# Attention projections placed by SyncE and ScalarE together, x tiles issued first, rows of minus one filled by Pool

## The chip, the core and the metric

The kernel runs on one core of a Trainium2 chip. The core has five engines that run their own instruction streams: TensorE (PE in the profile), VectorE (DVE), ScalarE (ACT), Pool (POOL) and SyncE (SP, which here only issues DMAs). A DMA that an engine issues stands in that engine's stream; the transfer itself is done by sixteen DMA engines that all issuers share. The metric is device time in microseconds of one execution, lower is better.

## What is computed

The reference chains four blocks over a hidden state of 2048 tokens by 1024 features, each with a layer norm before and behind it and a residual. The change is in the third, grouped-query causal attention over two sequences of 1024 tokens (b = 2, t = 1024). Cut to what matters:

```python
q = jnp.dot(x, Wq).reshape(b, t, H, HD).transpose(0, 2, 1, 3)
kv = jnp.dot(x, Wkv).reshape(b, t, G, 2, HD).transpose(2, 3, 0, 1, 4)
scores = jnp.einsum('bhqd,bhkd->bhqk', q, k)
scores = jnp.where(causal[None, None], -jnp.inf, scores)
weights = jax.nn.softmax(scores * (1.0 / HD ** 0.5), axis=-1)
ctx = jnp.einsum('bhqk,bhkd->bhqd', weights, v)
```

There are 32 query heads of 32 features and 8 key and value groups; the kernel works through 16 head groups of four query heads each, eight for either sequence. Everything is float32 in and out; products are made from a high and a low part of each operand, which is why each projected matrix exists as `qh` (high) and `ql` (low).

## The kernel before

The program is four stages (StageA to StageD) with a barrier of all engines between them. Each engine's stream is written out by hand, and waits are on counting semaphores (`Sig`). The third stage, StageC, is the one that the diff touches. It works like this.

**Opening.** SyncE loads sixteen x tiles (`sp_x`, L1638) into four buffers, tile u as soon as tile u-4's buffer is free. TensorE transposes each (L1762) and multiplies it for V (L1784 to L1786); ScalarE takes the high part (L1961) and copies V (L1967), VectorE makes the low part (L2119, L2122). Then come the projections, the `JOBS`: K0, K1, query groups 0, 1 and 2 ahead of the loop, the other fifteen (queries 3 to 15, K2, K3) inside it. A job has two parts of 512 columns. For a part TensorE does 24 matmuls (L1808 to L1810), ScalarE casts the high part into `c_qh` (L1974), VectorE writes the low part into `c_ql` or `c_cH` (L2131), and then the part has to be *placed*: 4 heads x 3 row blocks of 32 x 512 are copied by twelve DMAs into `c_K` (L1654) or `c_Q` (L1665), from where the heads' matmuls read them. Between jobs SyncE loads the next weights (`sp_w`, L1622), ScalarE casts them (L1943 in the opening, L1950 in quarters in the loop) and VectorE splits them (L2091, L2098).

Rows 96 of `c_K` must hold -1: VectorE writes them with two memsets (L2166, L2167) once V is complete, since the weights of V lie in the even heads of `c_K` until then; `c_K`'s row 96 times the stored row maximum in `c_Q` subtracts the maximum inside the score matmul.

**Maxima.** For each of 16 head groups o there are 48 maxima: a matmul (`pe_amax`, L1832) into one of three turning PSUM banks and a reduction on VectorE (L2142, L2146). The first 60 of them run while the last two projections of the opening do; the first waits until both parts of query group 0 and of K0 and K1 are placed.

**Loop.** 768 slots, 48 for each o. In slot S TensorE makes score S (`pe_score`, L1848) into one of three banks, maximum S+60, now and then three matmuls of a job, and a product with V (L1863); ScalarE makes the exponential (L2010) and frees the bank; Pool masks (L2225) and adds up rounds (L2240); VectorE does the maximum. A finished head is evacuated by ScalarE (L2023, L2028), and SyncE moves its sums through memory (`sp_finish`, L1682 to L1698) for a reciprocal on VectorE (L2151) and a multiplication on Pool (L2205). The table `JOBS` gives, for each job in the loop, the slots of its matmuls and the two slots from which its parts are placed; it is written by hand and the change doesn't touch it. The third stage's streams on SyncE and ScalarE are in `sp` and `act`.

An issue on SyncE or ScalarE waits for its semaphores in the stream of its engine, so what stands behind it waits too.

## Time and profile before

| | |
|---|---|
| median of 3 executions | 2426.3 us (2423.89 to 2428.33) |
| the profiled execution | 2424.34 us, span 2422.6 us |
| TensorE busy | 2162.4 us, 89% |
| VectorE busy | 1430.3 us, 59% |
| ScalarE busy | 918.8 us, 38% |
| Pool busy | 903.1 us, 37% |
| granted TensorE clock, mean | 0.947 |

Times in the rows are in us from the start of the span, durations in us or ns as marked. PE is TensorE's matmuls and PEld its weight loads, which overlap them; SPq and ACTq are DMAs issued by SyncE and ScalarE, where the duration is that of the issue and not of the transfer. The granted clock is a share of the full 2.4 GHz. A bracket behind a row is the engine's idle time before it and what ended it.

### The profile page before, as it was taken

To read this page: it belongs to the slowest core of one execution; us is meant where nothing else is said; L and a number is where in the kernel's file an instruction comes from. 1 tells how busy PE (TensorE), PEld (TensorE's weight loads), DVE (VectorE), ACT (ScalarE), POOL (GpSimd) and SP (SyncE) were. 2 spreads that over 40 slices of the span, in tenths; PEclk is the share of its full clock that TensorE was granted. 3 is DMA by queue.
4 is the path that set the end of the run, shared out by engine and by line. 5 is a ranking of instruction groups with operands and counts; after the bars stand their busy time and mean duration, and the time that the engine had idled before them with its cause. 6 is when DMAs were issued, how large, how long until landed. Compare 5 with 4: busy or idle time off the path is not lost.

```text
span 2422.6 us, 31281 instructions
## 1 busy us (share of the span) xinstructions
PE 2162.4 (89%) x11064; PEld 1530.2 (63%) x11064; DVE 1430.3 (59%) x3245; ACT 918.8 (38%) x1675; POOL 903.1 (37%) x761
## 2 busy tenths in 40 slices
PE   4899965699999978879999899999988699999998
PEld 4655534588888868755556555655543487667676
DVE  7866766577777653366766566676662156543333
ACT  4654643233332322215554455455555222221111
POOL 1344664444444420004565454556655222110000
PEclk9899987899999988979999999999987899999999
DMA  5220446112221127431223622322221544434332
GB/s 166 73 91 1 145 137 192 67 70 70 79 70 70 70 87 269 123 80 35 76 63 89 193 67 62 90 75 65 54 68 59 192 174 167 137 121 150 111 114 95
DMA packets 139570, 249.28 MB, mean 103 GB/s; under 512 B 26885, under 2 KB 69765, under 8 KB 139191
## 3 DMA queue, kind: packets, MB, share of 16 engines
q1 hardware_dynamic: 130711, 230.51, 30.1%
q10 hardware_dynamic: 8704, 16.78, 2.1%
q8 instruction: 88, 1.44, 0.3%
q14 instruction: 67, 0.55, 0.1%
HBM read 139.48 MB, written 76.02 MB: 89 GB/s over the span
## 4 chain that ended last, share of the span: by engine, by line
PE 62%; POOL 12%; DVE 10%; issue 5%; DMA 3%; ACT 3%; SPq 2%; POOLq 0%; DVEq 0%; ACTq 0%
POOL c_S L2240 10%; PE PS L2425 5%; PE PS L2382 4%; PE PS L2383 4%; PE PS L2386 4%; PE PS L1848 3%; PE PS L1069 3%; PE PS L1070 3%; PE PS L1071 3%; PE PS L1832 3%; PE PS L1863 3%; PE PS L1102 2%; PE PS L1104 2%; PE PS L1103 2%; DVE PS L2146 2%
## 5 line engine op out<-in xcount | busy, mean ns | idle before, releaser
L2010 ACT ACTIVATE c_P<-PS 128x512 f32<-128x512 f32 (+3 forms) x768 | 359.8, 495 | 366.9 <-PE PS L1848 338.0
L2240 POOL TENSOR_TENSOR c_S<-c_S,c_P 128x2048 f32<-128x2048 f32 (+6 forms) x111 | 317.0, 2864 | 73.7 <-DVE c_S L2112 66.6
L1832 PE MATMUL PS<-c_K,c_Q 96*128 96x512 f32 (+3 forms) x768 | 281.6, 377 | 45.9 <-DVE cst L2146 23.6
L1848 PE MATMUL PS<-c_Q,c_K 97*128 97x512 f32 (+3 forms) x768 | 284.5, 384 | 2.5 <-ACT c_P L2010 2.5
L1848 PEld LDWEIGHTS PS<-c_Q,c_K 97*128 97x128 f32 x768 | 149.9, 198 | 162.7 <-ACT c_P L2010 73.1
L2142 DVE TENSOR_REDUCE cst<-PS 128x1 f32<-128x512 f32 x256 | 176.1, 688 | 109.3 <-PE PS L1832 109.0
L1832 PEld LDWEIGHTS PS<-c_K,c_Q 96*128 96x128 f32 x768 | 152.1, 198 | 110.5 <-DVE cst L2146 57.6
L2225 POOL TENSOR_SCALAR_AFFINE_SELECT c_P<-c_P 128x512 f32<-128x512 f32 x128 | 81.6, 638 | 335.9 <-ACT c_P L2010 335.9
L1863 PE MATMUL PS<-c_P,c_V 128*32 128x512 f32 (+3 forms) x1536 | 172.3, 522 | 27.2 <-POOL c_P L2225 15.3
L2146 DVE CUSTOM_DVE_ANT_0 PS<-PS,maskw 128x128 f32<-128x128 f32 (+3 forms) x256 | 127.1, 505 | 85.3 <-PE PS L1832 83.9
L2382 PE MATMUL PS<-c_xth,d_xh 128*128 128x512 f32 x384 | 157.6, 410 | 19.2 <-DVE d_xl L2497 19.2
L2146 DVE CUSTOM_DVE_ANT_0 PS<-PS,maskw,cst 128x128 f32<-128x128 f32 (+3 forms) x256 | 142.9, 558 | 51.4 <-PE PS L1832 35.0
L199 POOL TENSOR_TENSOR maskw<-maskw,mhalf 128x1 f32<-128x1 f32 x64 | 36.6, 572 | 363.1 <-DVE maskw L168 363.1
L1069 PE MATMUL PS<-b_w13h,b_xsh 128*128 128x460 f32 (+1 forms) x384 | 149.0, 388 | 15.8 <-DVE b_xsl L1274 15.5
L1301 DVE SCALAR_TENSOR_TENSOR b_pr<-b_g,b_a 128x460 f32<-128x460 f32 x192 | 160.6, 872 | 1.6
L1193 ACT ACTIVATE b_g<-PS 128x460 f32<-128x460 f32 x96 | 52.9, 553 | 273.2 <-PE PS L1076 273.2
L2383 PE MATMUL PS<-c_xtl,d_xh 128*128 128x512 f32 x384 | 152.9, 398 | 0.0
L1395 POOL TENSOR_TENSOR b_gp<-b_g 128x230 f32<-128x230 f32 x96 | 84.8, 884 | 163.2 <-DVE b_g L1286 163.2
L1070 PE MATMUL PS<-b_w13l,b_xsh 128*128 128x460 f32 (+1 forms) x384 | 144.6, 376 | 0.0
L1071 PE MATMUL PS<-b_w13h,b_xsl 128*128 128x460 f32 (+1 forms) x384 | 143.7, 374 | 0.0
L1286 DVE TENSOR_TENSOR b_g<-b_g,PS 128x460 f32<-128x460 f32 x96 | 60.5, 630 | 117.2 <-ACT b_g L1193 117.2
L1808 PE MATMUL PS<-c_xth,c_wh 128*128 128x512 f32 x304 | 125.7, 414 | 4.2 <-DVE c_ql L2131 2.0
(282 smaller groups left out, 4844.1 us busy)
## 6 DMA issues: line engine op xcount, KB each, us to landing
a_xin<-in_x SPq DMA_DIRECT2D x32, 512.0 KB, 4.3
c_Q<-c_qh SPq DMA_DIRECT2D x256, 64.0 KB, 2.0
d_x<-scr SPq DMA_DIRECT2D x32, 512.0 KB, 3.9
scr<-a_xin SPq DMA_DIRECT2D x16, 512.0 KB, 5.5
scr<-a_hid SPq DMA_DIRECT2D x16, 512.0 KB, 3.0
b_xn<-scr SPq DMA_DIRECT2D x16, 512.0 KB, 5.7
b_x<-scr SPq DMA_DIRECT2D x16, 512.0 KB, 4.8
scr<-b_x SPq DMA_DIRECT2D x16, 512.0 KB, 2.6
```

Source lines behind the costliest of these rows:

```text
L1069: e.matmul(o, self.xsh[:, par, i, :], wh[:, v, i, :], start=i == 0, stop=False)
L1070: e.matmul(o, self.xsh[:, par, i, :], wl[:, v, i, :], start=False, stop=False)
L1071: e.matmul(o, self.xsl[:, par, i, :], wh[:, v, i, :], start=False, stop=False)
L1832: e.matmul(bank[:, 0:hi - lo], self.Q4[0:96, 4 * (o % 3) + g, 128 * t:128 * t + 128], self.K4[0:96, HEADS[o % 8], lo:hi], start=True, stop ...
L1848: e.matmul(self.k.bank(i % 3)[:, 0:hi - lo], self.K4[0:97, HEADS[o % 8], 128 * kt:128 * kt + 128], self.Q4[0:97, 4 * (o % 3) + g, lo:hi], ...
L1863: m = e.matmul(k.bank(5)[32 * g:32 * g + 32, lo - 512 * half:512], self.V[:, kt, o // 8, HEADS[o % 8], :], P[:, g, 0:hi - lo], start=kt == ...
L2010: e.activation(self.P[:, R % 3, g, 0:hi - lo], self.k.bank(i % 3)[:, 0:hi - lo], ACT.Exp, scale=SCALE).then_inc(self.exp_s.s, 1)
L2142: e.tensor_reduce(m, r, AX, ALU.max).then_inc(self.mx_s.s, 1)
L2146: e.tensor_tensor_reduce(out=r, in0=r, in1=self.maskw[:, 512 - n:512], scale=1.0, scalar=m if lo > 0 else -3.0e38, op0=ADD, op1=ALU.max, a ...
L2240: m = e.tensor_tensor(S[:, gs, 512 - n:512], S[:, gs, 512 - n:512], P[:, gs, 0:n], ADD)
L2382: e.matmul(o, h, wh[:, c, cols], start=c == 0, stop=False)
L2383: e.matmul(o, h, wl[:, c, cols], start=False, stop=False)
```

## The change

- SyncE issues x tile 15 and the weights for job 3 before it places any part of K0 (before, K0's first part stood between x tiles 14 and 15).
- A placement of a part is split for the jobs of the opening (n < 5) and for K2, 7, K3 and 11 in the loop: SyncE issues the six DMAs of heads 0 and 1, ScalarE the six of heads 2 and 3 (`place`, `act_place`, `shared`). The other jobs stay with SyncE. In the opening ScalarE issues the first part's six behind its cast of the second part, and the second part's six behind the next weights' cast; in the loop at the same slot as SyncE.
- The rows of minus one are written by Pool at the start of the stage (odd heads) and after V (even heads); SyncE's placement of K1 waits for V alone, and the first score waits for both memsets.

```diff
--- before.py
+++ after.py
@@ -1638,17 +1638,29 @@
         e.dma_start(self.xin[u % 4], self.xn_src[128 * t:128 * t + 128, :]).then_inc(self.k.ldx[u % 4].s, 16)
 
     def sp_place(self, e, n, part):
+        self.place(e, n, part, range(2) if self.shared(n) else range(4))
+
+    def act_place(self, e, n, part):
+        if self.shared(n):
+            self.place(e, n, part, range(2, 4))
+
+    @staticmethod
+    def shared(n):
+
+        return n < 5 or JOBS[n][0] in ("K2", 7, "K3", 11)
+
+    def place(self, e, n, part, heads):
         what = JOBS[n][0]
         c = slice(512 * part, 512 * part + 512)
         e.wait_ge(*self.qlo_s(2 * n + part + 1))
         if what in ("K0", "K1", "K2", "K3"):
             first = (1, 0, 0, 1)[int(what[1])]
             if what == "K1":
-                e.wait_ge(*self.given_s(3))
+                e.wait_ge(*self.vmm_s(16))
             elif what != "K0":
                 e.wait_ge(*self.score_s(192 if what == "K2" else 384))
                 e.wait_ge(*self.amax_s(192 if what == "K2" else 384))
-            for g in range(4):
+            for g in heads:
                 j, s = 2 * g + first, slice(32 * g, 32 * g + 32)
                 for r, q in ((0, self.qh[s, part, :]), (32, self.qh[s, part, :]), (64, self.low(n, part)[s, :])):
                     e.dma_start(self.K4[r:r + 32, j, c].bitcast(F32), q.bitcast(F32)).then_inc(self.k4[part].s, 16)
@@ -1659,7 +1671,7 @@
         if o >= 3:
             e.wait_ge(*self.score_s(48 * (o - 2)))
             e.wait_ge(*self.amax_s(48 * (o - 2)))
-        for g in range(4):
+        for g in heads:
             q, s = 4 * (o % 3) + g, slice(32 * g, 32 * g + 32)
             for r, x in ((0, self.qh[s, part, :]), (32, self.low(n, part)[s, :]), (64, self.qh[s, part, :])):
                 e.dma_start(self.Q4[r:r + 32, q, c].bitcast(F32), x.bitcast(F32)).then_inc(self.placed[part].s, 16)
@@ -1717,11 +1729,10 @@
             self.sp_x(e, u)
             if u == 11:
                 self.sp_w(e, 3)
-            if u >= 14:
-                self.sp_place(e, 0, u - 14)
         self.sp_w(e, 4)
-        for part in range(2):
-            self.sp_place(e, 1, part)
+        for n in (0, 1):
+            for part in range(2):
+                self.sp_place(e, n, part)
         self.sp_w(e, 5)
         for n in (2, 3):
             for part in range(2):
@@ -1843,6 +1854,8 @@
         i = 48 * o + 4 * r + g
         if r == 0 and g == 0:
             e.wait_ge(*self.mrow[o % 2](o // 2 + 1))
+        if i == 0:
+            e.wait_ge(*self.given_s(2))
         if i >= 3:
             e.wait_ge(*self.exp_s(i - 2))
         e.matmul(self.k.bank(i % 3)[:, 0:hi - lo], self.K4[0:97, HEADS[o % 8], 128 * kt:128 * kt + 128],
@@ -2040,16 +2053,21 @@
                 self.act_v(e, u - 3)
             if u in (12, 13):
                 self.act_job(e, 0, u - 12)
+            if u in (14, 15):
+                self.act_place(e, 0, u - 14)
             if 6 <= u < 14:
                 self.act_x1(e, 2 * u - 12)
                 self.act_x1(e, 2 * u - 11)
         for n in range(1, 5):
             for part in range(2):
                 self.act_job(e, n, part)
+                if part == 1:
+                    self.act_place(e, n, 0)
                 if n == 4 and part == 0:
                     self.act_mrow(e, 0)
             if n < 4:
                 self.act_w(e, n + 3)
+            self.act_place(e, n, 1)
         for o in range(16):
             for s, (r, g) in enumerate(SLOTS):
                 S = 48 * o + s
@@ -2064,6 +2082,8 @@
                     self.act_evac(e, 2 * o, 0)
                 if S in self.evac_at:
                     self.act_job(e, *self.evac_at[S])
+                if S in self.place_at:
+                    self.act_place(e, *self.place_at[S])
                 for n, q in self.split_at.get(S, ()):
                     self.act_w4(e, n + 1, q)
                 for q in range(4):
@@ -2157,15 +2177,11 @@
             if u == 0:
                 self.dve_w(e, 0)
                 self.dve_w(e, 1)
-                e.memset(self.maskw[:, 0:384], 0.0).then_inc(self.given_s.s, 1)
+                e.memset(self.maskw[:, 0:384], 0.0)
             if u in (6, 12):
                 self.dve_w(e, 2 if u == 6 else 3)
             if u in (12, 13):
                 self.dve_job(e, 0, u - 12)
-        e.wait_ge(*self.vmm_s(16))
-        e.memset(self.K4[96:97, 0:8:2, :].bitcast(F32), -1.0).then_inc(self.given_s.s, 1)
-        e.memset(self.K4[96:97, 1:8:2, :].bitcast(F32), -1.0).then_inc(self.given_s.s, 1)
-        e.wait_ge(*self.given_s(3))
         for n in (1, 2):
             for part in range(2):
                 self.dve_job(e, n, part)
@@ -2217,6 +2233,9 @@
     def pool(self, e):
 
         S, adds = self.S, 0
+        e.memset(self.K4[96:97, 1:8:2, :].bitcast(F32), -1.0).then_inc(self.given_s.s, 1)
+        e.wait_ge(*self.vmm_s(16))
+        e.memset(self.K4[96:97, 0:8:2, :].bitcast(F32), -1.0).then_inc(self.given_s.s, 1)
         for o in range(16):
             for r, (kt, lo, hi) in enumerate(ROUNDS):
                 P, n = self.P[:, (12 * o + r) % 3, :, :], hi - lo
```

Line numbers of the changed kernel are up to 19 higher; its placements are L1666 and L1677, its cast of `c_qh` L1987, its exponentials L2023.

SyncE's stream where the x tiles end and K0's first part is placed, before (`c_cH` and `c_cS` are two of the four x buffers here, `c_raw` the raw weights):

```order
L1638 DMA c_xin<-scr 128x1024 x2
L1638 DMA c_cH<-scr 128x1024
L1654 DMA c_K<-c_qh 32x512 x2
L1654 DMA c_K<-c_ql 32x512
L1654 DMA c_K<-c_qh 32x512 x2
L1654 DMA c_K<-c_ql 32x512
L1654 DMA c_K<-c_qh 32x512 x2
L1654 DMA c_K<-c_ql 32x512
L1654 DMA c_K<-c_qh 32x512 x2
L1654 DMA c_K<-c_ql 32x512
L1638 DMA c_cS<-scr 128x1024
```

and now:

```order
L1638 DMA c_xin<-scr 128x1024 x2
L1638 DMA c_cH<-scr 128x1024
L1638 DMA c_cS<-scr 128x1024
L1622 DMA c_raw<-in_wq 128x8x128
L1666 DMA c_K<-c_qh 32x512 x2
L1666 DMA c_K<-c_ql 32x512
L1666 DMA c_K<-c_qh 32x512 x2
L1666 DMA c_K<-c_ql 32x512
```

The last x tile and a weight load stand ahead of the placements, and a part is six issues instead of twelve.

ScalarE's stream at the end of the opening, before (`c_mT` are the transposed maxima of head group 0):

```order
L1974 CAST c_qh<-PS 128x512 x2
L1943 CAST c_wh<-c_raw 128x1024
L1974 CAST c_qh<-PS 128x512
L1980 CAST c_mT<-PS 32x128
L1974 CAST c_qh<-PS 128x512
L2010 ACT_TABLE_LOAD
L2010 ACTIVATE c_P<-PS 128x512 x4
```

and now:

```order
L1987 CAST c_qh<-PS 128x512
L1677 DMA c_Q<-c_qh 32x512
L1677 DMA c_Q<-c_ql 32x512
L1677 DMA c_Q<-c_qh 32x512 x2
L1677 DMA c_Q<-c_ql 32x512
L1677 DMA c_Q<-c_qh 32x512 x2
L1677 DMA c_Q<-c_cH 32x512
L1677 DMA c_Q<-c_qh 32x512 x2
L1677 DMA c_Q<-c_cH 32x512
L1677 DMA c_Q<-c_qh 32x512
L2023 ACT_TABLE_LOAD
L2023 ACTIVATE c_P<-PS 128x512 x4
```

Twelve issues, six for each part of query group 2, stand between the last cast and the table load of the first exponential; the same kind of six now stands ahead of each weight cast in the opening.

ScalarE's stream in the loop at K2, whose parts are placed from slots 217 and 227, now (before, no DMA stood in it):

```order
L1987 CAST c_qh<-PS 128x512
L2023 ACTIVATE c_P<-PS 128x512
L1666 DMA c_K<-c_qh 32x512 x2
L1666 DMA c_K<-c_ql 32x512
L1666 DMA c_K<-c_qh 32x512 x2
L1666 DMA c_K<-c_ql 32x512
L1963 CAST c_wh<-c_raw 128x256 x2
L2023 ACTIVATE c_P<-PS 128x384
L1963 CAST c_wh<-c_raw 128x256 x2
```

This is the second part: the quarters of the next weights' cast, which stood right behind the exponential, stand behind six issues.

## Rows read from the trace of the kernel before

**Rows 1.** Windows: engines' busy us and instructions, PEclk, DMA share, GB/s.

```profile
1000.00:1020.00 20.00, 20.00 (x90) 16.57 (x89) 9.07 (x6) 2.71 (x4) 0.00 (x0) 1.00 0.26 60
1020.00:1040.00 20.00, 6.62 (x31) 5.18 (x29) 2.61 (x3) 2.22 (x3) 0.00 (x0) 0.77 0.54 128
```

**Rows 2.** TensorE's timeline in the opening: start, us, engine, line, tiles.

```profile
986.90 1.97 PE L1762 MATMUL PS<-cst,c_cS 128*128 128x128 f32 x8 [6.72 <-DMA c_cS<-scr]
...
1039.97 0.77 PE L1832 MATMUL PS<-c_K,c_Q 96*128 96x128 f32 x2 [13.38 <-DMA c_Q<-c_qh]
```

**Rows 3.** SyncE's timeline in the opening.

```profile
983.32 0.58 SPq L1638 DMA_DIRECT2D c_cS<-scr  x1
...
1007.33 1.15 SPq L1654 DMA_DIRECT2D c_K<-c_qh  x2
...
1037.67 0.59 SPq L1665 DMA_DIRECT2D c_Q<-c_qh  x1
```

**Rows 4.** The view of L1665 alone: ns min/median/max, then landing.

```profile
L1665 SPq DMA_DIRECT2D c_Q<-c_qh x256: 507/591/1881, 1023.1 to 1778.6; - x128
...
DMA to landing us min/median/max: 1.9/2.0/5.3
```

**Rows 5.** VectorE's timeline in the opening.

```profile
984.77 0.69 DVE L2131 TENSOR_TENSOR c_ql<-PS,c_qh 128x512 fp32r<-128x512 f32 x1 [8.90 <-DMA c_K<-c_ql]
...
998.83 3.47 DVE L2166 MEMSET c_K<- 1x4096 f32 x1 [7.66 <-PE PS L1786]
...
1006.61 0.69 DVE L2131 TENSOR_TENSOR c_ql<-PS,c_qh 128x512 fp32r<-128x512 f32 x1
...
1054.14 1.22 DVE L2091 TENSOR_TENSOR c_wl<-c_raw,c_wh 128x1024 fp32r<-128x1024 f32 x1
...
1083.59 0.69 DVE L2131 TENSOR_TENSOR c_cH<-PS,c_qh 128x512 fp32r<-128x512 f32 x1
```

**Rows 6.** ScalarE's timeline in the opening.

```profile
960.64 1.01 ACT L1961 CAST c_xth<-PS 128x1024 fp32r<-128x1024 f32 x1 [7.93 <-PE PS L1762]
...
977.35 1.01 ACT L1961 CAST c_xth<-PS 128x1024 fp32r<-128x1024 f32 x1 [1.97 <-PE PS L1762]
...
1051.97 1.05 ACT L1943 CAST c_wh<-c_raw 128x1024 fp32r<-128x1024 f32 x1
...
1080.90 0.58 ACT L1974 CAST c_qh<-PS 128x512 fp32r<-128x512 f32 x1 [4.60 <-PE PS L1810]
...
1082.80 2.31 ACT L2010 ACTIVATE c_P<-PS 128x512 f32<-128x512 f32 x4
```

**Rows 7.** ScalarE's timeline in the loop.

```profile
1304.70 0.60 ACT L2010 ACTIVATE c_P<-PS 128x512 f32<-128x512 f32 x1 [0.30 <-PE PS L1848]
...
1308.25 0.60 ACT L2010 ACTIVATE c_P<-PS 128x512 f32<-128x512 f32 x1 [0.57 <-PE PS L1848]
...
1340.09 0.39 ACTq L1995 DMA_DIRECT2D c_xth<-x_d  x1
...
1558.33 0.59 ACT L2023 COPY c_cS<-PS 128x512 f32<-128x512 f32 x1 [0.35 <-PE PS L1890]
...
1575.47 0.60 ACT L2023 COPY c_cS<-PS 128x512 f32<-128x512 f32 x1
```

**Rows 8.** TensorE's timeline in the loop.

```profile
1323.20 0.50 PE L1832 MATMUL PS<-c_K,c_Q 96*128 96x512 f32 x1 [2.55 <-DVE cst L2146]
...
1544.70 0.50 PE L1808 MATMUL PS<-c_xth,c_wh 128*128 128x512 f32 x1 [1.45 <-DVE c_wl L2098]
```

**Rows 9.** SyncE's timeline in the loop.

```profile
1340.06 1.23 SPq L1665 DMA_DIRECT2D c_Q<-c_qh  x2
...
1357.88 0.51 SPq L1687 DMA_DIRECT2D cst<-sum_d  x1
```

**Rows 10.** VectorE's timeline in the loop.

```profile
1303.93 0.69 DVE L2131 TENSOR_TENSOR c_ql<-PS,c_qh 128x512 fp32r<-128x512 f32 x1 [0.69 <-ACT c_qh L1974]
...
1362.67 0.25 DVE L2151 RECIPROCAL cst<-cst 128x16 f32<-128x16 f32 x1 [6.27 <-DMA cst<-sum_d]
```

## The prediction

> **What bounds the kernel now.** The change touches the third of the kernel's four stages only, attention, which runs from about 905 to 1990 us of the span, so I read that stage alone, in four steps. First the windows of its opening part [rows 1]: TensorE is busy 20 of 20 us from 1000 to 1020, at a granted clock of 1.00, but 6.6 us in the 20 us after, where the clock sags to a mean of 0.77. Second TensorE's timeline [rows 2]: the first hole, 6.72 us, ends when an x tile lands (c_cS<-scr); the second, 13.38 us, ends when a placement lands (c_Q<-c_qh). Third SyncE's timeline [rows 3]: the x tile was issued at 983.32, behind twelve placements of K0, and from 1007.33 on SyncE does nothing but issue, back to back, until 1037.67. The view of the line [rows 4] has a median of 0.591 us for an issue and 2.0 us to landing; with the 0.04 us between issues that is 0.63 us each, and the 48 placements of that stretch are 30.3 us. So the opening is bound by one engine's issuing, not by transfers or arithmetic. Fourth VectorE and ScalarE in the same stretch [rows 5, 6], for what is late next. Behind the opening comes the loop of 768 scores. There ScalarE's exponentials wait for TensorE most of the time, and what matters is how long ScalarE can be held before TensorE runs out of its three score banks.
>
> **All x tiles first, and the rows of minus one on Pool.** x tile 15 needs the transposes of tile 11, which ScalarE picked up at 960.64 [rows 6], so it can be issued about 22 us earlier and the 6.72 us hole goes. What is late next: the low half of K0's second part, which VectorE may write only when the first part's twelve placements have landed (984.77 before, [rows 5]); the last two x splits stand behind it on VectorE. SyncE now places its six from 973.9; ScalarE's six start once its cast of tile 14 is dispatched (977.35, [rows 6]): the sixth starts 5 x 0.63 = 3.2 us later, at 980.5, and lands at 982.6. I take 983.6, because SyncE's first issues there were slow while x stores ran. Then V tile 14 starts at 985.5 and V tile 15 waits for a V copy that now stands behind ScalarE's six issues of K0's second part (984.3 + 3.8 = 988.1): V is done at 991.6. Before, VectorE's first memset marks that moment: 998.83 [rows 5]. Gain so far 7 us. The two memsets are 3.47 us each on VectorE, between V and the low half of K1 (1006.61, [rows 5]); on Pool they have idle time and nobody asks for them until the first score, some 70 us later. Without them that low half starts as soon as TensorE and ScalarE have K1, at 997: 9.6 us earlier.
>
> **Half the placements on ScalarE, in the opening.** SyncE needs 3.8 us for a part instead of 7.6 and is no longer last. Last is now ScalarE's own queue, since its weight cast and its next cast stand behind its issues. TensorE's parts take 5.4 us (24 matmuls at 20 us / 90, [rows 1]): K1 from 992.1 ends at 1002.9, query group 0 at 1013.8. ScalarE: six of group 0's first part 1013.9 to 1017.7, weight cast, six of the second part 1017.7 to 1021.5, the last started at 1020.9 and landed at 1022.9. SyncE's chain ends before: its six of the second part are out at 1019.5. I take 1023.5 for the first maximum, because two issuers at once raise the DMA share, which is 0.54 in the last window already with one issuer [rows 1]. Before 1039.97 [rows 2]. **Gain 16.5 us**; bounds 12 (landings 2 us later and each weight load 1 us) and 19 (issues on ScalarE at the 0.39 us of [rows 7] instead of 0.59). With only some 3 us idle ahead of it TensorE should keep its full clock: **gain 1.5 us** (0 to 2), VectorE's waits for it in the four us behind 1039.97.
>
> From there VectorE is the bound (60 maxima of about 0.65 us), and two new waits appear. (a) ScalarE's cast of weight 6 (1051.97, [rows 6]) now stands behind six issues; VectorE's split of the same weight (1054.14, [rows 5]) then starts 1.05 us after a cast that is 3.8 us late, of which 1.1 us plus the time VectorE gains is slack: **cost 2.3 us** (0 to 3.8). (b) The first exponential. ScalarE's last cast is at 1080.90 [rows 6]; behind it now stand six issues (to 1084.7), a wait for VectorE's low half (1083.59 + 0.69, [rows 5]), six more (to 1088.5), and only then the table load and the first exponential: 1089.8 where it was 1082.80 [rows 6]. TensorE has three banks of scores and then stands. Of the 7.0 us I give back 0.5, as the clock was low there before too: **cost 6.5 us** (4 to 7).
>
> **Half the placements on ScalarE, in the loop.** Four jobs, K2, 7, K3, 11, two parts each. At K2's first part the low half is there at 1304.62 [rows 10]; six issues hold ScalarE to 1308.5. The exponential that started at 1304.70 [rows 7] ends at 1309.1, and the score that needs its bank was started about 1307.8, half a us before its exponential at 1308.25 [rows 7]: 1.3 us lost. Job 7's and K3's first parts meet later demand: 0 and 0.1. At the second parts of K2 and K3 the weight casts stand right behind the issues, and TensorE was already waiting for VectorE's splits (1323.20 with 2.55 us, 1544.70 with 1.45 us, [rows 8]); they move by 3.8 us less what VectorE wins when Pool's adds are over: 2.6 and 3.2. Job 11's first part falls on the evacuation of a finished head (1558.33, [rows 7]), which starts 3.8 us later, and the bank's next user waits: 2.5. At its second part ScalarE is itself the last (evacuation at 1575.47, [rows 7]) and would go on at 1580.1: 4.4. Against them stands a gain at job 7's second part. SyncE there issues twelve placements and only then the small load of the sums, at 1357.88 [rows 9], and VectorE waits 6.27 us for it, to 1362.67 [rows 10]. Issued at 1353.3 it lands by 1358.1, about when VectorE comes: gain 4.5 us. **Sum of the loop: cost 1.3 + 2.6 + 0 + 0.1 + 3.2 + 2.5 + 4.4 - 4.5 = 9.6 us**; bounds 2 (cheap issues, exponentials catch up) and 16 (Pool's chain of adds is pushed too).
>
> **Sum.** -16.5 - 1.5 + 2.3 + 6.5 + 9.6 = +0.4 us. The profiled execution itself took 2424.3 us with a span of 2422.6, which is 2.0 below the median of 2426.3; on the median: 2426.7, rounded 2426.5.
>
> The Trainium skill (DMA: Bandwidth & Descriptors, "Issuing engines are not separate DMA queues") says that issuing from several engines saves only the sequencer's time, "which is usually small relative to the DMA itself". By that rule the split is worth nothing in the opening and the sum would be +18.4 instead of +0.4, which rival 3 below stands for; here the sequencer's time is what ends last (48 x 0.63 us against 2.0 us to landing), so the trace speaks for the split.
>
> **Rivals.** (1) *Faster: ScalarE's issues are cheap or hidden.* ScalarE's own loads from memory take 0.39 us each [rows 7]; at 0.43 with the gap, six are 2.6 us. Then the first maximum comes 2.5 us earlier, the weight cast costs 1.2 less, the first exponential 1.6 less (it still waits for the low half at 1084.3), the loop 6.0 less: 11.3 in all, 2415. It decides from about 0.5 us an issue downwards, or where a head's slack takes up the stalls. Against it: SyncE has 0.32 us for isolated x loads and yet 0.59 for placements.
>
> (2) *Slower: the loop pays more than the opening wins.* One mechanism: ScalarE late in the second half of a head delays Pool's adds, which run back to back there, and the delay is never made up. It decides when the hold exceeds the 3 us that three banks cover. K2 and K3 then cost 3 us more each, and crowded landings put the first maximum 3 us later: 2435.5.
>
> (3) *It does not do what it says: the two issuers take turns.* If one descriptor generator is held by one issuer at a time, the 48 placements still take 30.3 us, only 9 us earlier (gain 10 with the clock), each hold of ScalarE lasts 7.6 us, and job 7's gain goes: about 2466. The trace speaks against it: a ScalarE issue at 1340.09 of 0.39 us [rows 7] lies inside SyncE's pair at 1340.06 [rows 9], and neither is longer than usual. The Trainium skill (Perfetto Trace Analysis, "DMA Instruction - HWDGE (DVE, Sync)") has it that way, a block locked for exclusive use; by that rule this rival holds, by the rows it does not.
>
> **How the numbers follow.** The forecast holds 0.39 (its own range 2422 to 2431); rival 1 has 0.34, rival 2 0.24, rival 3 0.03. A measurement of this kernel can tell about 0.2%, 4.9 us, from no change, so rival 1 is the chance of faster, the forecast that of no change, rivals 2 and 3 that of slower. The range goes to rival 1's time less 2 and rival 2's plus 1.5: 2413 to 2437, and leaves out rival 3 and the tails.
>
> **What would show it.** x tile 15's hole gone and V ended near 991; first maximum near 1023 with under 4 us of TensorE's wait; the first exponential right behind a block of twelve ScalarE issues, near 1073.6 of the span (1082.8 - 18.0 + 8.8); six issues in a row on ScalarE at 0.63 us and a hole on TensorE behind them at K2 and job 11; VectorE's wait of 6.27 us for the sums gone. Wrong would be: ScalarE's issues under 0.5 us, landings well over 2 us, or the score loop (first exponential to last) shorter than before.

## The result and the profile after

The changed kernel takes 2443.36 us (median of 6 runs, 2440.4 to 2447.06) against 2425.5 us before (6 runs, 2420.34 to 2428.33): a ratio of 1.0076 with an interval of 1.0063 to 1.0089, so it is slower by 17.9 us. The forecast was 2426.5 with a range of 2413 to 2437: the time lies 6.4 us above the range. The profiled execution has a span of 2442.0 us against 2422.6.

Three points in time, each the start of one instruction of ScalarE, and the end of the span split the 19.4 us between the two spans. "x tile 11" is ScalarE's cast of that tile, the last point that both kernels reach by the same instructions but for Pool's memset of the odd rows [rows 6].

| us | before | after | change of the stretch that ends there |
|---|---|---|---|
| x tile 11 | 960.64 | 962.34 | +1.7 |
| first exponential | 1082.80 | 1083.35 | -1.15 |
| last exponential | 1891.10 | 1910.27 | +18.6 |
| end of the span | 2422.6 | 2442.0 | +0.2 |

All of the loss that the change makes lies in the loop of 768 exponentials; the 1.7 us ahead of x tile 11 are less than what profiled executions differ by there (see Experiments). Inside the second stretch the first maximum (VectorE's start of it) went from 79.8 to 69.8 us behind x tile 11, a gain of 10.0 us, and the way from there to the first exponential gave 8.8 us of it back.

Windows of the opening, after (the columns are those of rows 1):

```profile
1000.00:1020.00 20.00, 20.00 (x90) 16.57 (x89) 3.72 (x5) 3.40 (x5) 0.00 (x0) 1.00 0.49 118
1020.00:1040.00 20.00, 11.95 (x45) 9.22 (x43) 8.18 (x21) 1.63 (x2) 0.00 (x0) 0.74 0.46 113
...
988.00:991.00 3.00, 3.00 (x19) 3.00 (x19) 0.55 (x1) 0.37 (x1) 0.00 (x0) 0.61 0.85 200
...
1024.00:1031.00 7.00, 0.00 (x0) 0.00 (x0) 1.92 (x2) 0.75 (x2) 0.00 (x0) 0.66 0.69 177
1031.00:1036.00 5.00, 4.30 (x12) 3.56 (x12) 2.63 (x9) 0.00 (x0) 0.00 (x0) 0.50 0.20 46
```

TensorE's timeline, after (start, us, engine, line, tiles; in brackets the idle time before and what ended it). The first row answers to the first of rows 2, the second to the second; the others are new holes in the loop, beside rows 8:

```profile
987.47 0.38 PE L1795 MATMUL PS<-c_K,c_xth 128*128 128x256 f32 x1 [1.85 <-DVE c_xtl L2142]
...
1031.70 0.76 PE L1843 MATMUL PS<-c_K,c_Q 96*128 96x128 f32 x2 [8.05 <-DMA c_Q<-c_qh]
...
1309.32 0.66 PE L1861 MATMUL PS<-c_Q,c_K 97*128 97x512 f32 x1 [1.73 <-ACT c_P L2023]
...
1327.69 0.37 PE L1849 MATMUL PS<-cst 128*32 128x128 f32 x1 [5.31 <-DVE cst L2166]
...
1361.90 0.58 PE L1843 MATMUL PS<-c_K,c_Q 96*128 96x256 f32 x1 [4.28 <-DVE cst L2166]
...
1572.97 0.80 PE L1843 MATMUL PS<-c_K,c_Q 96*128 96x512 f32 x1 [3.08 <-ACT c_cS L2036]
...
1597.17 0.47 PE L1843 MATMUL PS<-c_K,c_Q 96*128 96x128 f32 x1 [4.50 <-ACT c_cS L2036]
```

The x tile's hole of 6.72 us is gone, the one ahead of the first maximum shrank from 13.38 to 8.05 us, and the holes in the loop stand behind blocks of ScalarE's issues, the two named after VectorE by way of the weight casts that VectorE waits for. That is what ScalarE's timeline shows, after (ACTq rows are its DMA issues; the rows answer to rows 6 and 7):

```profile
1014.28 0.61 ACTq L1666 DMA_DIRECT2D c_K<-c_cH  x1
1014.99 0.59 ACT L1987 CAST c_qh<-PS 128x512 fp32r<-128x512 f32 x1 [3.09 <-issue]
1018.96 0.59 ACT L1987 CAST c_qh<-PS 128x512 fp32r<-128x512 f32 x1 [3.38 <-DMA c_K<-c_cH]
...
1026.31 0.61 ACTq L1677 DMA_DIRECT2D c_Q<-c_qh  x1
...
1082.05 1.28 ACT L2023 ACT_TABLE_LOAD   x1 [7.02 <-issue]
1083.35 1.09 ACT L2023 ACTIVATE c_P<-PS 128x512 f32<-128x512 f32 x2
...
1304.28 1.43 ACTq L1666 DMA_DIRECT2D c_K<-c_qh  x2
1305.73 0.97 ACTq L1666 DMA_DIRECT2D c_K<-c_ql  x1
1306.73 1.26 ACTq L1666 DMA_DIRECT2D c_K<-c_qh  x2
1308.01 0.61 ACTq L1666 DMA_DIRECT2D c_K<-c_ql  x1
1308.67 2.07 ACT L2023 ACTIVATE c_P<-PS 128x512 f32<-128x512 f32 x4 [4.65 <-issue]
...
1325.49 0.71 ACT L1963 CAST c_wh<-c_raw 128x256 fp32r<-128x256 f32 x2 [4.55 <-issue]
```

**How the loop is read below.** Each slot has one exponential, so its start, measured from the first one, can be set beside the same slot of another kernel, and the difference is what was lost up to there. For the eight places, after against before, with the size that the forecast had:

| place (slot) | forecast | lost |
|---|---|---|
| K2 first (217) | 1.3 | 3.5 |
| K2 second (227) | 2.6 | 2.9 |
| 7 first (242) | 0 | 0 |
| 7 second (250) | -4.5 | -0.4 |
| K3 first (414) | 0.1 | 0.6 |
| K3 second (424) | 3.2 | 3.6 |
| 11 first (437) | 2.5 | 6.2 |
| 11 second (453) | 4.4 | 6.3 |
| sum | 9.6 | 22.7 |

From 22.7 go 0.9 us by which the kernel was ahead at slot 217, some 1.0 us that come back by slot 482 and 2.2 us behind slot 672, to the 18.6 of the first table. The last 2.2 us say nothing of the change: behind slot 672 the kernel before is itself slow in its profile, and the kernels below whose loop is as before the change gain 3.4 to 3.7 us on it there.

### The profile page after: what moved, and what is told of

Its sections match the earlier page's. It is cut to its first block, busy times and chain, and to the rows that moved or that the text cites. A ratio compares the mean times of both kernels' runs of the same rounds, so it can differ in the third digit from the quotient of the medians.

```text
span 2442.0 us, 31293 instructions
## 1 busy us (share of the span) xinstructions
PE 2172.1 (89%) x11064; PEld 1535.6 (63%) x11064; DVE 1422.3 (58%) x3243; ACT 918.5 (38%) x1675; POOL 909.9 (37%) x763
## 4 chain that ended last, share of the span: by engine, by line
PE 62%; POOL 12%; DVE 10%; issue 5%; DMA 3%; ACT 3%; ACTq 2%; SPq 1%; POOLq 0%; DVEq 0%
POOL c_S L2259 10%; PE PS L2444 4%; PE PS L2401 4%; PE PS L2402 4%; PE PS L2405 4%; PE PS L1861 3%; PE PS L1843 3%; PE PS L1069 3%; PE PS L1070 3%; PE PS L1071 3%; PE PS L1876 3%; PE PS L1102 2%; PE PS L1819 2%; PE PS L1104 2%; PE PS L1103 2%
## 5 line engine op out<-in xcount | busy, mean ns | idle before, releaser
L2023 ACT ACTIVATE c_P<-PS 128x512 f32<-128x512 f32 (+3 forms) x768 | 358.7, 495 | 366.3 <-PE PS L1861 327.1
L2401 PE MATMUL PS<-c_xth,d_xh 128*128 128x512 f32 x384 | 157.5, 410 | 19.8 <-DVE d_xl L2516 19.8
```

What stands on the lines that cost most here:

```text
L2023: e.activation(self.P[:, R % 3, g, 0:hi - lo], self.k.bank(i % 3)[:, 0:hi - lo], ACT.Exp, scale=SCALE).then_inc(self.exp_s.s, 1)
L2401: e.matmul(o, h, wh[:, c, cols], start=c == 0, stop=False)
```

## Experiments

Times are medians beside runs of the kernel before on the same chip; "behind x tile 11" takes off what the stages ahead of the change vary by (956.6 to 967.9 us of the span in the profiles, though the kernels have the same instructions up to there but for Pool's first memset and one small memset of the holds). The loop varies too: the kernels below whose loop is as before the change have 803.7 to 808.4 us from first to last exponential in their profiles. So a difference in the loop is read over the slots beside the edit and not from its whole length.

### Which part of the change does what

```diff
     def shared(n):
-        return n < 5 or JOBS[n][0] in ("K2", 7, "K3", 11)
+        return n < 5                                # opening
+        return JOBS[n][0] in ("K2", 7, "K3", 11)    # loop
+        return False                                # neither
+        return n < 3                                # K0, K1, group 0
```

Each kernel has one of the four lines. The x tiles first and the memsets on Pool stay in all four.

> Placements are split in the opening alone (n < 5); in the loop SyncE issues all twelve of a part again. Theory A (ScalarE's six issues of 3.7 to 4.7 us hold the exponentials in the loop): from the first to the last exponential the loop is as before the change again, about 18.6 us shorter than in the changed kernel, and the time is 2424 to 2426, no better than before the change, because the opening wins 10 us at the first maximum and gives 9 back by the first exponential. Rival B (two issuers at once slow the landings wherever they meet, and the weights' loads with them): the loop recovers less than 10 us and the time stays over 2432. Rival C (x tiles first, or Pool's memsets, cost the time): 2440 or more, since both are still in.

> Placements are split in the loop alone (K2, 7, K3, 11); in the opening SyncE issues all twelve, x tiles still first and memsets still on Pool. Theory A: the loop loses the same 18 to 22 us as in the changed kernel, slot by slot (3.5 behind slot 217, 3 behind 227, 3.6 behind 424, 6 each behind 437 and 453); the time is that of the kernel without any split plus about 20, 2435 to 2440. Rival B: the loss in the loop is the same, since both issuers meet there too, so this run tells A and B apart only by whether VectorE and TensorE wait for a landing or for ScalarE. Rival C: over 2443.

> No placement is split; what is left of the change is x tiles first and the memsets on Pool. Theory A: SyncE's 48 placements of 0.63 us start 6 to 8 us earlier than before the change, no wait is added on ScalarE, the loop is as before: 2417 to 2420. Rival B: also 2417 to 2420, and less than the kernel that is split in the opening alone by over 10 us. Rival C: 2425 or more.

> Placements are split for K0, K1 and query group 0 alone (n < 3), the 24 + 24 + 24 that the first maximum waits for. Theory A: first maximum as in the kernel split in the opening (about 1030 on the clock of the kernel before), but neither the 3.2 us ahead of weight 6's cast nor the 7.0 us ahead of the first exponential: 8 to 9 us less than that kernel, 2414 to 2417. Rival B: crowded landings eat the gain, 2420 or more. Rival C: 2425 or more.

| shared | median us | ratio to before, interval | first maximum behind x tile 11 | first exponential behind it | loop |
|---|---|---|---|---|---|
| kernel before | 2422.83 | 1 | 79.8 | 122.2 | 808.3 |
| neither | 2417.8 | 0.9982, 0.9969 to 0.9995 | 76.0 | 118.5 | 805.3 |
| opening | 2422.72 | 1.000, 0.9985 to 1.0015 | 68.6 | 119.6 | 808.4 |
| loop | 2439.47 | 1.0075, 1.0049 to 1.0102 | 76.5 | 117.8 | 823.8 |
| K0, K1, group 0 | 2409.73 | 0.9946, 0.9927 to 0.9965 | 68.7 | 110.3 | 803.7 |

Three of the four times are as theory A expected or within 2 us of it; that of the three shared jobs is 4 us below its 2414 to 2417, about the 4.7 us by which its loop is shorter than that of the kernel shared in the opening, a difference that no edit makes.

The whole loss comes with the sharing in the loop. In the opening, x tiles and memsets alone bring the first exponential 3.7 us forward; sharing K0, K1 and group 0 brings 8.2 us more; sharing groups 1 and 2 as well takes 9.3 us away again and moves the first maximum by nothing. ScalarE's timeline shows where 7.0 of these 9.3 us are. With the whole opening shared:

```profile
1081.10 1.28 ACT L2023 ACT_TABLE_LOAD   x1 [7.03 <-issue]
1082.39 1.57 ACT L2023 ACTIVATE c_P<-PS 128x512 f32<-128x512 f32 x3
```

and with three shared jobs:

```profile
1068.79 0.59 ACT L1987 CAST c_qh<-PS 128x512 fp32r<-128x512 f32 x1 [4.61 <-PE PS L1821]
1069.39 1.28 ACT L2023 ACT_TABLE_LOAD   x1
1070.68 1.57 ACT L2023 ACTIVATE c_P<-PS 128x512 f32<-128x512 f32 x3
```

From the last cast to the first exponential it is 1.89 us here and 8.91 there (cast at 1073.48). The other 2.3 us are already there at the last cast, and the weight cast that stands behind six issues is the nearest cause: VectorE's split of weight 6 starts 85.3 us behind x tile 11 with the whole opening shared and 82.8 us with three shared jobs, 2.5 us later.

### Why the first maximum came at 1032 and not at 1025

Group 0's last issue starts at 1026.31 in the changed kernel. Its transfer lands at 1031.46, 5.15 us later, and TensorE starts at 1031.70, 5.4 us later; rows 4 have a median landing of 2.0. The load of a weight (512 KB) was issued at 1025.45, 0.86 us ahead of that issue. With three shared jobs the same load has the same place, 0.85 us ahead of ScalarE's last issue. The edit moves it behind group 1's first part,

```diff
         for n in (2, 3):
             for part in range(2):
                 self.sp_place(e, n, part)
-            self.sp_w(e, n + 4)
+                if n == 3:
+                    self.sp_w(e, 6 + part)
```

on top of the three shared jobs:

> As e4, but the load of weight 6 (512 KB), which SyncE issued between group 0's last transfers and ScalarE's, is issued after group 1's first part. Theory A (the transfers landed 5 us after their issue because they share the DMA engines with that load): group 0's last transfer lands some 2 us after its issue, the first maximum comes 2.5 to 3.5 us earlier (1029.1 to about 1026), the first exponential as much or a little less, 2407 us. Rival (two queues landing at once are slower by themselves): the first maximum stays at 1029 and the time at 2410.

Measured: 2407.63 us, ratio 0.9937 (0.992 to 0.9953). The first maximum comes 66.2 us behind x tile 11 in place of 68.7, the first exponential 107.7 in place of 110.3. ScalarE's last issue and TensorE's first maximum, with the load 0.85 us ahead of that issue (the profile names a placement from `c_ql` as the releaser; the last of group 0 to land, at 1028.39, is this one):

```profile
1023.68 0.61 ACTq L1677 DMA_DIRECT2D c_Q<-c_qh  x1
...
1028.63 0.77 PE L1843 MATMUL PS<-c_K,c_Q 96*128 96x128 f32 x2 [6.89 <-DMA c_Q<-c_ql]
```

and with the load later:

```profile
1020.02 0.61 ACTq L1677 DMA_DIRECT2D c_Q<-c_qh  x1
...
1022.33 0.77 PE L1844 MATMUL PS<-c_K,c_Q 96*128 96x128 f32 x2 [4.40 <-DMA c_Q<-c_qh]
```

From issue to release it is 4.95 us with the load just ahead and 2.31 without, though both engines issue placements in both kernels. So it is the load, and not the two queues, that makes these landings slow. The whole time's gain over three shared jobs (2.1 us by the medians) is inside both intervals, and the loop of this profile is 806.8 us, 3.2 longer than with three shared jobs; the trace of the opening is what decides.

The kernel before had such a case: its placement at 1023.13, issued 0.68 us behind the load at 1022.45, landed after 3.96 us.

### What a hold of ScalarE costs in the loop

All on top of the three shared jobs (loop 803.7 us, no hold in it). The loop's four jobs are shared again, but with one head instead of two on ScalarE (three transfers a part) and three on SyncE:

```diff
-            self.place(e, n, part, range(2, 4))
+            self.place(e, n, part, range(2, 4) if n < 3 else range(3, 4))
```

> ScalarE places half for K0, K1 and group 0, as in e4; in the loop's four near projections it takes one head only (3 transfers a part, SyncE 9). Theory A (a hold of ScalarE costs the loop what it exceeds the slack of the three score banks by): a hold of about 1.9 us instead of 3.8 stays within the stretch that the banks cover, so the loop loses 1 to 5 us of the 18.6 it lost with two heads, 2410 to 2415 us in all. Rival B (each transfer on ScalarE costs its own 0.64 us, whatever the slack): half of 18.6, so 9 to 10 us, 2419 us. Rival C (the loss comes from landings that change their order, not from the hold): the loss stays near 18, 2428 us.

Measured: 2415.14 us, ratio 0.9973 (0.9959 to 0.9987); the loop is 813.5 us, 9.9 longer, of which 1.8 stand ahead of the first place, so 8.1 are left for the eight places. It is 5.4 us slower than the three shared jobs by the medians. Neither expectation holds cleanly: A's upper end (5) is passed, and B's 9 to 10 is what the whole loop shows, but its time of 2419 did not come. Then only group 11 shared, with two heads:

```diff
-        return n < 3
+        return n < 3 or JOBS[n][0] == 11
```

> As e4, and ScalarE takes half of group 11's placements, six at slots 437 and 453. Theory A: each hold of ScalarE there stands for itself and costs what it did with all four projections shared, 6 us each, 12 us in all, 2421 to 2422 us. Rival (the loss at group 11 was the sequel of those before it): clearly less, 2413 to 2416 us.

Measured: 2419.62 us, ratio 0.9988 (0.9976 to 0.9999). Between slots 432 and 492 the exponentials lose 9.5 us, and 11.1 us between the same slots in the changed kernel. So most of the loss there stands for itself; 1.6 us can be a sequel of the places before. Next a hold without any transfer, by twenty, then forty one-column exponentials into a tile of their own (all of the loop's placements are SyncE's again):

```diff
-                if S in self.place_at:
-                    self.act_place(e, *self.place_at[S])
+                if S in (437, 453):
+                    for n in range(40):
+                        e.activation(self.junk[:, n + 1:n + 2], self.junk[:, 0:1], ACT.Exp)
```

> As e4, all placements of the loop on SyncE, but ScalarE is held at slots 437 and 453 by twenty exponentials of one column each, about 4 us and no transfers, where e8 held it by six transfers. Theory A (the hold of the exponentials is the whole cost): the loop loses 8 to 11 us as in e8, 2419 us. Rival (the transfers from two queues or their order do it): it loses under 4 us, 2411 to 2414 us.

> As e10, with forty one-column exponentials at each of the two slots: e10's twenty held ScalarE for 1.98 us and the exponentials between slots 432 and 492 lost 2.3 us for both together; forty should hold it for some 3.9 us, as e8's six transfers did. Theory A (only the length of the hold counts, and what passes the slack of the score banks is paid in full, with the banks' return behind it): 7 to 10 us lost between slots 432 and 492, as the 9.4 us in e8. Rival (the transfers of the second queue did a share of e8's loss by themselves): 5 us or less.

Measured: 2419.0 us with twenty (ratio 0.9983, 0.9972 to 0.9994) and 2423.5 in the one run with forty, beside 2419.06. The first time meets theory A's 2419 by accident: the profile with twenty reaches x tile 11 at 967.91, 7.5 us later than the three shared jobs do, and loses only 2.4 us at group 11. By its loss that run falls to the rival ("under 4 us"), but it doesn't test what was meant, since twenty exponentials hold ScalarE for 2.0 us and not the 4 expected; with forty the hold is 3.8 us and the loss 7.8, theory A's 7 to 10. Why the whole time is 9 us above that of the three shared jobs stays open, so these two are read by slots alone. Last, ScalarE's six issues moved three slots later, behind the evacuation of the finished head:

```diff
-                if S in self.place_at:
-                    self.act_place(e, *self.place_at[S])
+                if S - 3 in self.place_at:
+                    self.act_place(e, *self.place_at[S - 3])
```

> As e8 (half of group 11's placements on ScalarE), but ScalarE issues its six three slots later, at slots 440 and 456, behind the evacuation of the finished head that stands at slots 438 and 454. In e8 TensorE ran on for 3 us beside the hold and then waited 3.08 us for the bank that the evacuation of the sums (c_cS) frees, and not for a score bank. Theory A (what is late is the evacuation's bank): the hold now meets only the three score banks, which cover 2 to 3 us, and the loss between slots 432 and 492 falls from 9.5 to 1 to 5 us; time 2412 to 2416 us. Rival (any hold of 4 us is paid in full wherever it stands): 8 to 10 us again, 2419 us.

Measured: 2412.46 us, ratio 0.9949 (0.9932 to 0.9965), against 0.9988 with the six in their old place. All five kernels at group 11, against the three shared jobs:

| at slots 437 and 453 | ScalarE held, us | next exponential late by, us | lost from slot 432 to 492 |
|---|---|---|---|
| 20 one-column exponentials | 2.0, 2.0 | 1.4, 1.9 | 2.4 |
| 3 transfers | 2.5, 2.7 | 2.2, 2.8 | 4.1 |
| 40 one-column exponentials | 3.8, 3.8 | 3.2, 3.7 | 7.8 |
| 6 transfers | 4.5, 4.6 | 4.1, 4.7 | 9.5 |
| 6 transfers, three slots later | 4.5 at slot 440, 1.9 at 456 | 4.0 at 441, 2.1 at 457 | 1.6 |

The loss goes with the length of the hold, whether transfers fill it or not; and the same transfers cost 1.6 us instead of 9.5 once the evacuation stands ahead of them. The first hold is as long there and is made up: of its 4.0 us, 2.9 are back by slot 443. The second is shorter, since part of the issues runs beside exponentials. ScalarE's timeline with six transfers:

```profile
1550.55 0.61 ACTq L1677 DMA_DIRECT2D c_Q<-c_qh  x1
1551.26 0.59 ACT L2036 COPY c_cS<-PS 128x512 f32<-128x512 f32 x1 [4.45 <-issue]
```

with forty exponentials:

```profile
1551.44 3.84 ACT L2088 ACTIVATE c_junk<-c_junk 128x1 f32<-128x1 f32 x40
1555.16 0.58 ACT L2037 COPY c_cS<-PS 128x512 f32<-128x512 f32 x1
```

and three slots later, where the wait that the profile names is TensorE's and the issues stand ahead of its end (the line before the issues is an exponential):

```profile
1552.94 0.59 ACT L2036 COPY c_cS<-PS 128x512 f32<-128x512 f32 x1 [0.35 <-PE PS L1903]
...
1554.72 0.54 ACTq L1677 DMA_DIRECT2D c_Q<-c_qh  x1
...
1559.69 1.10 ACT L2023 ACTIVATE c_P<-PS 128x256 f32<-128x256 f32 x4 [4.53 <-PE PS L1861]
```

TensorE is what tells the places apart. Its timeline with six transfers:

```profile
1548.54 0.28 PE L1861 MATMUL PS<-c_Q,c_K 97*128 97x256 f32 x1
1551.90 0.80 PE L1843 MATMUL PS<-c_K,c_Q 96*128 96x512 f32 x1 [3.08 <-ACT c_cS L2036]
1552.49 0.63 PE L1819 MATMUL PS<-c_xth,c_wh 128*128 128x512 f32 x1
```

with forty exponentials:

```profile
1555.79 0.51 PE L1844 MATMUL PS<-c_K,c_Q 96*128 96x512 f32 x1 [2.25 <-ACT c_cS L2037]
1556.14 0.40 PE L1820 MATMUL PS<-c_xth,c_wh 128*128 128x512 f32 x1
```

The bank it waits for is a maximum's, kept until ScalarE has evacuated the sums (c_cS), and not one of the three score banks. Behind the hole of 3.08 us the same matmul takes 0.63 us instead of 0.40, at a mean granted clock of 0.59 in the four us from 1552 on; behind that of 2.25 us the next matmul still takes 0.40, but the clock falls there too, to a mean of 0.68 from 1556 to 1560. Three slots later TensorE has no such wait: in its list of waits from 1548 to 1603 the largest is 2.0 us for c_P, in two pieces.

### The wait for the sums at group 7

SyncE issues group 7's second part ahead of the load of the sums [rows 9, 10]. Slot 253 in place of 250 puts the load first:

```diff
-(7, q_slots(231, 1, 241, 1), (242, 250))
+(7, q_slots(231, 1, 241, 1), (242, 253))
```

> As e4, with no split in the loop; group 7's second part is placed at slot 253 in place of 250, so that SyncE issues the load of the sums (slot 252) ahead of the twelve transfers. Theory A (VectorE's wait of 6.27 us for the sums of the kernel before is SyncE's queue, and TensorE's banks wait for it): the wait goes and the loop is 3 to 5 us shorter than e4's 803.65, 2406 us. Rival (something else comes last there, as VectorE's weight pieces): under 1 us, 2409 to 2410.

Measured: 2410.8 us, ratio 0.9949 (0.9931 to 0.9967), the loop 808.1 us. Against the three shared jobs the exponentials win 8.2 us between slots 252 and 268, and by slot 288 all of it and 2.4 us more are lost again. The expected 2406 us with a shorter loop did not come. SyncE's timeline of this kernel:

```profile
1350.93 0.58 SPq L1622 DMA_DIRECT2D c_raw<-in_wq  x1
1351.56 0.62 SPq L1702 DMA_DIRECT2D rec_d<-cst  x1
1363.67 0.32 SPq L1706 DMA_DIRECT2D c_cS<-rec_d  x1
```

Pool's:

```profile
1367.80 1.28 POOL L2221 TENSOR_TENSOR c_cH<-c_cH,c_cS 128x512 f32<-128x512 f32 x1 [19.82 <-DMA c_cS<-rec_d]
1369.03 9.18 POOL L2259 TENSOR_TENSOR c_S<-c_S,c_P 128x2048 f32<-128x2048 f32 x2
```

and ScalarE's:

```profile
1373.64 0.49 ACT L2023 ACTIVATE c_P<-PS 128x384 f32<-128x384 f32 x1 [8.09 <-POOL c_S L2259]
```

The store of the reciprocals is issued 0.63 us behind a 512 KB load, and the step that waits for it comes 12.1 us later; Pool then stands 19.8 us, and the exponentials 8.1 us for Pool. The wait removed on VectorE came back as a wait of ScalarE.

That load is not alone. From 1347.01 to 1360.46 ScalarE issues eight loads of x (`x_d`, 512 KB each), the weight's load itself lands after 12.0 us, and the DMA engines are counted as fully busy (the share is the last column but one):

```profile
1351.00:1364.00 13.00, 12.47 (x73) 6.72 (x74) 10.71 (x29) 8.87 (x18) 0.00 (x0) 1.00 1.06 331
```

What of the 12.1 us the weight's load makes and what the loads of x isn't told apart by any run. The last kernel puts both the second part and that load behind the four steps of `sp_finish` (slots 248 to 259), and takes the late load of the opening along:

```diff
-(7, q_slots(231, 1, 241, 1), (242, 250))
+(7, q_slots(231, 1, 241, 1), (242, 260))
...
-                    if q == 3:
+                    if q == 3 and S != 253:
                         self.sp_w(e, n + 2)
+                if S == 260:
+                    self.sp_w(e, JOB[7] + 3)
```

> The late load of weight 6 (as in e6) and, in the loop, group 7's second part and the 512 KB load of the weights after it placed at slot 260, behind the four steps that finish a kernel of the softmax sums (slots 248 to 259); no split in the loop. In e7 the sums' load went ahead, VectorE's banks came 6.9 us earlier, but the store of the reciprocals, issued 0.6 us behind the weight load, landed 12 us later and Pool's additions and the exponentials waited for that. Theory A (that landing took back what e7 had gained): with the load behind the four steps both waits are gone and the gain at slot 264 stays, the loop 3 to 6 us shorter than e6's 806.8, 2402 to 2405 us. Rival (the twelve transfers or the load now collide with the next kernel's steps): gain under 1 us or a loss, 2407 to 2412 us.

Measured: 2404.85 us, ratio 0.9926 (0.9912 to 0.9941), the lowest median of all, though its interval overlaps that of the late load alone (0.992 to 0.9953). The time is in the expected range, the loop is not: 804.3 us, 2.5 and not 3 to 6 shorter than the late load's. The store now goes out at 1340.26, ahead of the weight's load and of ScalarE's next load of x (1341.76), and SyncE's timeline has its answer back in 3.7 us:

```profile
1340.26 0.32 SPq L1702 DMA_DIRECT2D rec_d<-cst  x1
1343.92 1.71 SPq L1706 DMA_DIRECT2D c_cS<-rec_d  x4
```

Of the gain (8.2 us at slot 268 here too) 1.5 us are left at slot 280 and 3.5 at slot 300. Where it goes is one step further on. The twelve placements of group 7's second part, issued from 1345.74 to 1352.66, now go out beside the loads of x and land late (the view of their line from 1345.7 to 1353):

```profile
DMA to landing us min/median/max: 5.4/6.8/6.9
```

The last of them lands at 1359.51, and TensorE's first maximum of group 7, which needs it, starts then:

```profile
1359.60 0.45 PE L1846 MATMUL PS<-c_K,c_Q 96*128 96x128 f32 x1 [3.05 <-issue]
```

And the weight's load at 1353.30 now stands 0.63 us ahead of the store of the next head's sums, whose answer takes 8.4 us (1353.93 to 1362.32), so that VectorE waits 3.53 us for the next reciprocal. So the rival of this run (the transfers or the load collide with the next steps) holds in part.

At slot 432 the kernel is 5.9 us ahead of the one with the late load alone, and 2.5 at the last slot; against the three shared jobs, whose loop is 803.7 us, nothing is left at the last slot. What goes behind slot 672 (3.5 us against the late load, 3.8 against three shared jobs) goes where the kernel before is slow in its profile too; its cause stays open. That the edits at group 7 make the kernel faster as a whole is not shown.

## Why the prediction was wrong

The forecast of +0.4 us was -9.2 for the opening and +9.6 for the loop. Measured were -1.15 and +18.6, and 1.9 us outside both. So 8.0 us are missing in the opening (6.5 up to the first maximum, 1.5 of the clock) and 9.0 in the loop.

**x tiles first, memsets on Pool: right in kind, a third too large.** The hole is gone and V ends 4.65 us earlier (last copy of V at 995.00 against 997.95, less 1.7), where 7 was forecast; K1's low half comes 6.4 us earlier (1001.88 in place of 1006.61) and not 9.6. V's last two tiles went at a granted clock of 0.61 and then 0.82 (windows from 988 and from 991) behind the 1.85 us hole; the forecast had reckoned full speed there. It also took VectorE's memset at 998.83 for the end of V, 0.9 us behind the last copy. And its 997 for the low half does not follow from its own terms: K1 from 992.1 with 5.4 us for a part and the cast behind it gives 998 or later; measured, the low half starts 6.4 us behind K1's first matmul (995.51), which from 992.1 is 998.5.

**First maximum: the step that failed most is the landing beside a weight's load.** Forecast 16.5 us earlier, measured 10.0. The last issue started at 1026.31, which is 1024.6 without the 1.7 us of the stages ahead, against a forecast of 1020.9: 3.7 late. K1's first matmul was 1.7 late because V ended late, the matmuls up to group 0's end took 0.3 more than forecast, and the issues themselves 0.3. The other 1.4 us are ScalarE's cast of group 0's second part (1018.96), which waited for a placement of K1: issued at 1014.28, 1.1 us behind the weight's load at 1013.19, it landed after 4.6 us. From the last issue to the maximum the forecast allowed 2.6 us and it took 5.4: 2.8 late. So 4.2 of the missing 6.5 us are landings beside a load. The forecast had the risk as its bound ("landings 2 us later and each weight load 1 us", 12 us), and the measured 10.0 lies below even that; the late load shows what one load costs there, 2.6 us from issue to release (4.95 against 2.31).

**Clock: wrong.** TensorE stood 8.05 us and not 3, and the granted clock was 0.50 from 1031 to 1036, the lower of its two levels (1.2 of 2.4 GHz). The 1.5 us did not come. That 3 us of standing would have kept the clock was not tested here; in the loop it did not: behind the hole of 3.08 us that ends at 1572.97 the clock was 0.50 from 1573 to 1577.

**(a) and (b): right within half a us.** 2.3 and 6.5 us were forecast, 8.8 together, and the way from the first maximum to the first exponential grew by 8.8. Undoing both together gives 9.3, of which 7.0 are (b) by the distance from cast to exponential and 2.3 are left for (a).

**Loop: mechanism right, three terms too small and one missing gain.** 9.6 us were forecast with a bound of 16, and 22.7 less 4.1 came. The three terms are 7.8 us too small together, and the gain is short by 4.1. K2's second part, K3's second and the two that cost nothing hold within 0.5 us (1.2 us together). K2's first part was taken as 1.3 and cost 3.5: TensorE came to stand 1.73 us for a bank of an exponential (1309.32) and went on at a clock of 0.69 (window 1308 to 1312). Group 11's parts were taken as 2.5 and 4.4 and cost 6.2 and 6.3. The forecast had named the evacuation's bank for the first of them and charged 2.5 us of a hold of 3.8. The hold is 4.45 us at the first part and 4.85 at the second, from the exponential before it, because the part's low half comes first and the second of ScalarE's issues takes 0.87 us. TensorE then stands 3.08 and 4.50 us, and behind both holes it goes at the lower clock (0.50 in the windows from 1573 and from 1597), which the forecast had not charged. With forty exponentials (3.8 us, the hold that was forecast) the two parts cost 7.8 us together, near the 6.9 of the forecast; with 4.5 us it is 9.5, and in the changed kernel 11.1 between the same slots.

**Group 7's gain: the wait that ends last was the wrong one.** The wait of 6.27 us did go, but VectorE came to the reciprocal only at 1368.19. Its timeline, after:

```profile
1360.69 0.43 DVE L2118 TENSOR_TENSOR c_wl<-c_raw,c_wh 128x256 fp32r<-128x256 f32 x1 [3.56 <-ACT c_wh L1963]
...
1368.19 0.24 DVE L2171 RECIPROCAL cst<-cst 128x16 f32<-128x16 f32 x1
```

It waited 3.56 us for the quarters of the weight's cast, which stood behind the six issues on ScalarE, and 2.72 us for TensorE behind them. The forecast charged K2 and K3 for that chain and left it out at group 7, where the sums' wait had hidden it. A gain of 4.5 us became 0.4.

**Rivals.** Rival 2 (slower, 2435.5) was nearest in size and place. Its crowded landings (first maximum 3 us later) came, 2.8 us behind the last issue and 1.4 ahead of it. Its example for the loop, Pool's additions, did not: over the loop the exponentials wait 24.2 us for them, 25.6 us before, and the new holes end with ScalarE's evacuation, casts or exponentials. Rival 1 fell with its premise: ScalarE's issues take 0.61 us and not 0.39. Rival 3 is refuted: at 1304.28 the two engines issue at the same instant and only ScalarE's second and third issue are longer, 0.88 and 0.97 us, together 0.6 us of six. The +18.4 that the forecast gave for a split worth nothing in the opening is near what was measured by luck: the opening won 1.15 us, and it is the loop that cost 18.6.

The Trainium skill (DMA: Bandwidth & Descriptors, "Issuing engines are not separate DMA queues") fares in two parts. That the engines' queues feed shared DMA engines is what the late landing shows (4.95 against 2.31 us). That the issuing saved is usually small does not hold here: sharing three jobs' issues brings the first exponential 8.2 us forward.

## What to carry to other kernels

A DMA issue on a computing engine costs what stands behind it in that engine's stream: split placements where the engine would have waited anyway (here K0, K1, group 0: -8.2 us), and not where a cast, an evacuation or the first step of the next phase follows at once (+9.3 us for two groups, +18.6 us for eight parts in the loop, with holds up to 4.9 us). If it must be there, put it behind the copy that frees another engine's bank: three slots made 1.6 us of 9.5. A transfer on a critical path shouldn't be issued next to a 512 KB load: in the opening, holding the load back by a part gave 2.6 us. After removing a wait ask which transfer now meets it; at group 7 each of two attempts moved the collision by one step.

## What the runs showed of the hardware that was not expected

- Landing of a 64 KB placement is 2.0 us in the median, but 4.5 to 5.15 us when a 512 KB load was issued 0.85 us before it (opening: the changed kernel 5.15, sharing in the opening 4.5, three shared jobs 4.7), and 5.4 to 6.9 us beside ScalarE's loads of x, 512 KB each (last kernel, 1345 to 1353).
- A small store that shares the DMA engines with several such loads (share 1.06) came back after 12.1 us; the same store ahead of them came back after 3.7 us.
- Six back-to-back issues hold ScalarE 3.8 us by themselves and 4.5 us from the end of its last work. When SyncE and ScalarE start a block in the same instant, the second issue of one of them is longer: ScalarE's with 0.86 to 1.08 us in most blocks of the loop, SyncE's with 0.85 us in the second part of group 11 with one head.
- In the stages ahead of the change the profiled executions differ by up to 11 us (x tile 11 at 956.63 to 967.91) with all but the same instructions; in the loop the same slots agree to 0.1 us over long stretches, with single steps of 1 to 2 us and up to 3.8 us between slots 672 and 767. Comparing slot by slot told apart what the whole times could not.
